# Linear attention, gated FFN and softmax attention on one core: another order of GpSimd's, SyncE's and VectorE's work at the borders of the stages

## The chip, the cores and the metric

One core of one Trainium2 chip. The metric is device microseconds of one execution of the whole program, as the median of several runs. Engines: TensorE (PE; PEld is its weight load), VectorE (DVE), ScalarE (ACT), GpSimd (POOL), SyncE (SP), which here only issues DMAs.

## What is computed

x has shape (8, 1024, 256). Four blocks follow each other, each with a residual: linear attention with 16 heads (softplus features, running sum of k v), an FFN, softmax attention with ALiBi bias and causal mask, the same FFN again. The FFN is one recurrent cell over the batch index, then a projection:

```python
x = x + linear_attention(layernorm(x))
x = x + ffn(layernorm(x))
x = x + softmax_attention(layernorm(x))
x = x + ffn(layernorm(x))

def ffn(x):                       # scan over x.shape[0] = 8 "steps", batch by batch
    for xt in x:                  # c: state, (1024, 256)
        ft = sigmoid(xt @ wf.T + c @ uf.T + bf)
        it = sigmoid(xt @ wi.T + c @ ui.T + bi)
        gt = tanh(xt @ wc.T + c @ uc.T + bc)
        c = ft * c + it * gt
    return tanh(x @ wo.T + c_final @ uo.T + bo)
```

The state c is carried from batch to batch, and what the FFN adds to any batch needs the state after the last one.

## The kernel before

There are two halves, "phase 1" (linear attention and first FFN) and "phase 2" (softmax attention and second FFN). Each is a software pipeline over the 8 batches: a stage is one value of b (from -2 to 8) and has 144 steps k. In stage b, attention runs on batch b, the projections of queries, keys and values on batch nb = b + 1, the FFN (output projection, second layer norm, gates of the recurrent cell) on batch pb = b - 1, and the first layer norm on batch fb = b + 2. Each engine has its own program with a fixed order, written out by hand; engines meet only at semaphores. An engine that waits holds up all that is behind it in its order.

Products are done in bf16 parts: a "high" part and a "low" part, which is the fp32 value less its high part. GpSimd makes most of the low parts, and they are what this change moves:

- `state_low` (L1630 to L1633): the low part of the state, 128x2048, after ACT's `state_high` (L1011, L1013). PE's first gate product of the next stage, at k = 68, waits for it (`state_split`).
- `chunks_low(b, half)` (L1654 to L1660): the low part of half of batch b's attention output, 128x1024. The second half waits for the last chunk, which DVE divides at k = 142 of stage b (`take_chunk`, L1376). PE wants it at k = 13 of stage b + 1, where it turns the attention output for the projection (L539).
- `layer_norm` (L1700): GpSimd's normalisations (L1696) and their low parts (`ln_low`, L1717). In phase 1 the second layer norm and the first of batches 0 and 1 are normalised by DVE (L1391), and GpSimd makes the low parts alone; in phase 2 it is batch 0 whose first layer norm is normalised by DVE.
- `split_q` (L1662), the masked queries of linear attention; `sum_h`, `add_h` (L1641, L1647), which add the first FFN to x at the start of phase 2, with a tanh of ACT between them (`tanh_h`, L1024); `qk_low` (L1676, L1678), parts of queries and keys; `split_max` (L1687, L1691), parts of the softmax maxima.

At the end of a stage DVE does, in this order, the division of the last chunk (L1376) and the gates of the last group (`gates`, L1230: L1236, L1238, L1240, each over 128x512 with two inputs in SBUF), then the masks of the next chunk's scores (L1356) and a copy of the turned layer norm (L1349). ACT does `state_high` at k = 143, once the gates are through, and then its own copy of the turned layer norm (L1073), for which PE waits with the next turning (both parts use the same two banks). GpSimd's order over a stage of phase 1:

```python
for b in range(-2, B + 1):
    nb, pb, fb = b + 1, b - 1, b + 2
    # chunks_low(pb, 1); layer_norm(1, 1) if fb == 1; split_q(nb, 0); layer_norm(1, 2, XR, pb);
    # split_q(nb, 1); layer_norm(1, 1, XA, fb); chunks_low(b, 0);
    # state_low(1, pb) if pb < B - 1       <- waits for the end of the stage
```

The last stage of phase 1, b = 8, has only the FFN of batch 7: turned attention output, projection, statistics (L1519), normalisation (L1391), four `ln_low`, then on DVE the splitting of two weights (`split_weights`, L1318 to L1323), gates, and the state's part of h (L559, L1280). Then DVE sets the state anew for the second FFN (`set_state`, L1325 to L1331: memset, two additions, cast, difference) and takes the statistics of batch 0 of phase 2 (L1481), whose additions GpSimd has done meanwhile (L1647).

In stage b = -1 of phase 2, PE projects queries, keys and values of batch 0 (L882, L893), ACT puts them into a two-row buffer (`qk_in`, L1112), GpSimd splits each row (`qk_low(0, r)`, r = 0 to 3), SP stores them to DRAM (`store_qk`) and loads them back as stacks of heads (`load_group(gg)`, four DMAs of 256 KB, L393). At k = 96 the scores of the first group begin: PE makes them (L716, L692) and DVE takes the maxima (L1409), 36 units a group; `combine` (L1416) closes a group, at k = 131 for group 0, then come `split_max`, a turning (L774), a copy and four small DMAs (L1101), and at k = 0 of stage 0 the exponentials of group 0 can begin. There PE also turns the layer norm of batch 1 (`turns`, L539), for which it waits until GpSimd's `ln_low` of batch 1 is through. SP's queue is in order too: `load_h` fetches what the first FFN has left of a batch's h and waits for `add_h` two chunks before; `load_x1(fb)` waits for the layer norm of batch fb - 1.

Of the kernel before, what the change touches and what calls it, by code (L numbers as in the profile page):

```python
# [13 lines left out]
B, T, D = 8, 1024, 256  # L14
# [118 lines left out]
def mixer_kernel(nc, x, weights, cols, rows, key_rows, masks, out):  # L133
    with ExitStack() as ctx:
# [165 lines left out]
        def _(sp):  # L300
# [161 lines left out]
            for b in range(-2, B + 1):  # L462
# [5 lines left out]
                if batch_in(b + 1):  # L468
                    store_qk(b + 1, 0)
                    store_qk(b + 1, 1)  # L470
                if batch_in(b + 2):
                    load_h(b + 2, 2)
                    load_h(b + 2, 3)
                if b == -1:
                    load_group(0)
                if b == B:
                    for n in (3, 4, 5):
                        load_final(n)
                if batch_in(b - 1):
                    store_residual(2, b - 1)  # L480
                if b == B:
                    for n in (1, 6):
                        load_final(n)
                if batch_in(b):
                    load_group(GROUPS * b + 3)
                if batch_in(b):
                    load_residual(2, b)
                if batch_in(b + 2):
                    sp.wait_ge(sem["h_added"], 4 * (b + 3))
                    sp.dma_start(tokens(x2_dram, b + 2), XA[:, :, :]).then_inc(sem["x2_out"], 16)  # L490
                if batch_in(b - 1):
                    store_xw(b - 1)
                if batch_in(b + 1) and b >= 0:
                    load_group(GROUPS * (b + 1))
                if batch_in(b + 1):
                    store_qk(b + 1, 2)
                    store_qk(b + 1, 3)
                if b == -1:
                    load_group(1)
                if batch_in(b + 3):  # L500
                    load_x1(b + 3)
                    load_h(b + 3, 0)
                    load_h(b + 3, 1)
# [490 lines left out]
        def _(act):  # L994
# [120 lines left out]
            def fill_softmax(b, k):  # L1115
# [7 lines left out]
                if batch_in(fb) and k in (5, 9, 33, 37) and (fb or k > 9):  # L1123
                    tanh_h(fb, (5, 9, 33, 37).index(k))
# [99 lines left out]
        def _(dve):  # L1224
# [236 lines left out]
            def fill_softmax(b, k):  # L1461
# [15 lines left out]
                if batch_in(fb):  # L1477
                    if 62 <= k < 70:
                        if k % 2 == 0:
                            dve.wait_ge(sem["h_added"], 4 * fb + (k - 62) // 2 + 1)  # L1480
                        i = dve.bn_stats(ST[:, k - 62, :], XA[:, k - 62, :])  # L1481
                        if k == 69:
                            step(i)
# [352 lines left out]
```

## Time and profile before

| | |
|---|---|
| median of 3 runs | 2644.91 us (2637.34, 2644.91, 2654.23) |
| the profiled execution's own time | 2651.77 us |
| its span, first to last instruction | 2649.9 us |
| TensorE busy | 2178.3 us, 82% |
| VectorE busy | 1706.4 us, 64% |
| ScalarE busy | 1256.1 us, 47% |
| GpSimd busy | 782.9 us, 30% |
| mean granted TensorE clock | 0.920 |

The runs differ by 0.6% among themselves. Times in rows are us from the start of the span. Phase 1 lasts until about 1078, phase 2 from there.

### The profile page before, as it was taken

To read this page: it belongs to the slowest core of one execution; us is meant where nothing else is said; L and a number is where in the kernel's file an instruction comes from. 1 tells how busy PE (TensorE), PEld (TensorE's weight loads), DVE (VectorE), ACT (ScalarE), POOL (GpSimd) and SP (SyncE) were. 2 spreads that over 40 slices of the span, in tenths; PEclk is the share of its full clock that TensorE was granted. 3 is DMA by queue.
4 is the path that set the end of the run, shared out by engine and by line. 5 is a ranking of instruction groups with operands and counts; after the bars stand their busy time and mean duration, and the time that the engine had idled before them with its cause. 6 is when DMAs were issued, how large, how long until landed. Compare 5 with 4: busy or idle time off the path is not lost.

```text
span 2649.9 us, 58583 instructions
## 1 busy us (share of the span) xinstructions
PE 2178.3 (82%) x24832; PEld 1226.0 (46%) x24832; DVE 1706.4 (64%) x3811; ACT 1256.1 (47%) x2025; POOL 782.9 (30%) x658
## 2 busy tenths in 40 slices
PE   3568988979898787478799989898999889988964
PEld 1346555655656554233244444444444434443432
DVE  5646565564655534477687687776877877677327
ACT  2414334243443221126566666666656656665623
POOL 2223331333231111352344243351532422312110
PEclk8789999899899897769899999999999999998977
DMA  3201020111101102243123132231332302213053
GB/s 94 64 17 49 17 65 17 49 33 33 49 1 49 33 17 72 79 118 101 55 81 113 43 109 76 81 113 34 97 98 58 105 25 73 73 34 103 27 222 127
DMA packets 133172, 179.29 MB, mean 68 GB/s; under 512 B 10752, under 2 KB 96768, under 8 KB 132912
## 3 DMA queue, kind: packets, MB, share of 16 engines
q1 hardware_dynamic: 128816, 175.02, 21.5%
q8 instruction: 196, 3.21, 0.5%
q10 hardware_dynamic: 4096, 0.53, 0.1%
q14 instruction: 64, 0.52, 0.1%
HBM read 97.40 MB, written 77.59 MB: 66 GB/s over the span
## 4 chain that ended last, share of the span: by engine, by line
PE 61%; DVE 22%; ACT 7%; issue 3%; ACTq 3%; POOL 2%; DMA 1%; SPq 0%; DVEq 0%; POOLq 0%
PE general L573 10%; PE general L882 9%; PE out_of_heads L760 9%; DVE maxima L1409 7%; PE scores L716 6%; PE general L559 4%; PE general L893 3%; ACTq L1101 3%; PE general L539 3%; PE turned_scores L730 3%; PE out_of_heads L647 3%; PE out_of_heads L657 2%; PE scores L605 2%; PE general L547 2%; ACT probs_turned L1080 1%
## 5 line engine op out<-in xcount | busy, mean ns | idle before, releaser
L1409 DVE TENSOR_REDUCE maxima<-scores 128x1 f32<-128x512 f32 (+3 forms) x1536 | 793.0, 552 | 314.2 <-PE scores L692 199.2
L1080 ACT ACTIVATE probs_turned<-turned_scores 128x512 f32<-128x512 f32 x1152 | 678.6, 601 | 476.3 <-PE turned_scores L692 206.7
L716 PE MATMUL scores<-k_stacks,q_stacks 59*128 59x512 bf16 (+3 forms) x1536 | 455.3, 343 | 81.1 <-DVE maxima L1409 75.0
L730 PE MATMUL turned_scores<-q_stacks,k_stacks 61*128 61x512 bf16 (+3 forms) x1536 | 446.2, 336 | 56.2 <-ACT probs_turned L1080 56.0
L716 PEld LDWEIGHTS scores<-k_stacks,q_stacks 59*128 59x128 bf16 x1536 | 126.0, 96 | 323.8 <-DVE maxima L1409 240.7
L1717 POOL TENSOR_TENSOR ln_low<-ln 128x512 bf16<-128x512 f32 x128 | 138.9, 1094 | 284.8 <-DVE ln L1391 261.7
L1696 POOL TENSOR_SCALAR ln<-x_for_attention,ln_mean_var,ln_rstd 128x256 f32<-128x256 f32 x104 | 128.4, 1246 | 204.6 <-DVEq L1488 114.1
L730 PEld LDWEIGHTS turned_scores<-q_stacks,k_stacks 61*128 61x128 bf16 x1536 | 127.3, 95 | 111.1 <-ACT probs_turned L1080 76.7
L1632 POOL TENSOR_TENSOR state_low<-state_doubled,state_high 128x2048 bf16<-128x2048 f32 x14 | 57.0, 4069 | 379.7 <-ACT state_high L1013 379.7
L760 PE MATMUL out_of_heads<-probs_turned,values_odd_and_heads_out 128*17 128x512 f32 (+3 forms) x1536 | 162.0, 518 | 1.3 <-ACT probs_turned L1080 1.3
L1007 ACT ACTIVATE gate_tanhs<-general,feature_vectors 128x512 f32<-128x512 f32 x96 | 66.0, 688 | 204.4 <-PE general L573 200.1
L760 PE MATMUL out_of_heads<-probs_turned,values 128*17 128x512 f32 (+3 forms) x1536 | 160.6, 514 | 0.0
L1374 DVE TENSOR_SCALAR reciprocals<-scores 128x16 f32<-128x16 f32 x64 | 11.1, 173 | 226.3 <-PE scores L665 226.3
L1048 ACT COPY values_odd_and_heads_out<-out_of_heads 128x512 f32<-128x512 f32 x64 | 37.5, 586 | 235.5 <-PE out_of_heads L657 233.8
L882 PE MATMUL general<-ln_turned_high,w_high 64*128 64x512 bf16 (+1 forms) x600 | 124.9, 381 | 24.8 <-ACT qk_block L1112 7.8
L692 PE MATMUL scores<-mask_scores,identity_halves_swapped 64*128 64x128 bf16 (+1 forms) x640 | 137.7, 215 | 0.0
L692 PE MATMUL scores<-mask_scores,identity 64*128 64x128 bf16 (+1 forms) x640 | 137.5, 215 | 0.0
L692 PE MATMUL turned_scores<-mask_turned,identity 64*128 64x128 bf16 (+1 forms) x640 | 135.3, 211 | 0.0
L692 PE MATMUL turned_scores<-mask_turned,identity_halves_swapped 64*128 64x128 bf16 (+1 forms) x640 | 135.2, 211 | 0.0
L1687 POOL CAST maxima_parts<-maxima 128x16 bf16<-128x16 f32 x64 | 10.6, 198 | 387.7 <-DVE maxima L1416 387.7
L882 PE MATMUL general<-ln_turned_low,w_high 64*128 64x512 bf16 (+1 forms) x600 | 123.8, 377 | 0.0
L882 PE MATMUL general<-ln_turned_high,w_low 64*128 64x512 bf16 (+1 forms) x600 | 123.4, 377 | 0.0
(240 smaller groups left out, 5512.8 us busy)
## 6 DMA issues: line engine op xcount, KB each, us to landing
x_after_attention<-x_residual SPq DMA_DIRECT2D x16, 1024.0 KB, 5.2
x_times_wo<-x_wo_out SPq DMA_DIRECT2D x64, 256.0 KB, 2.1
q_stacks<-q_stack SPq DMA_DIRECT2D x64, 256.0 KB, 4.6
k_stacks<-k_stack SPq DMA_DIRECT2D x64, 256.0 KB, 4.8
x_for_attention<-in_x SPq DMA_DIRECT2D x8, 1024.0 KB, 5.6
x_residual<-in_x SPq DMA_DIRECT2D x8, 1024.0 KB, 5.4
x_for_attention<-x_after_attention SPq DMA_DIRECT2D x8, 1024.0 KB, 5.6
ffn_h<-x_times_wo SPq DMA_DIRECT2D x32, 256.0 KB, 6.0
```

The costliest lines, as they stand in the source:

```text
L539: mm = pe.transpose(bank[:, :].bitcast(BF16)[:, n * P:(n + 1) * P], src, ident[:, :])
L559: mm = pe.matmul(bank[:, n * D:(n + 1) * D], src[xp][:, k, at], W[wp][:, m, k, :], start=(i == 0), stop=(i == len(todo) - 1))
L573: mm = pe.matmul(bank[:, :], W[wp][:, m, k, e * P:(e + 1) * P], src[xp][:, k, c * CH:(c + 1) * CH], start=(n == 0), stop=(n == len(todo) - 1))
L692: return pe.matmul(columns[:, first:last + 1:step, :], eye, m, start=False, stop=(n == 1))
L716: mx = pe.matmul(bank_s[:, first * P:(first + tiles) * P], QS[at_s:at_s + QROWS, r, i * P:(i + 1) * P], KS[at_s:at_s + QROWS, r, k0 * P:(k ...
L730: ex = pe.matmul(bank_t[:, first * P:(first + tiles) * P], KS[at_t:at_t + KROWS, r, j * P:(j + 1) * P], QS[at_t:at_t + KROWS, r, i0 * P:(i ...
L760: mm = pe.matmul(OB[half][32 * g:32 * g + HV, at:at + tiles * P], values[:, j, HV * h:HV * (h + 1)], PR[:, (HEADS * unit + g) % SLOTS, fir ...
L882: return pe.matmul(bank[:, :], W[wp][rows_, m, k, e * P:(e + 1) * P], src[xp][rows_, k, c * CH:(c + 1) * CH], start=start, stop=stop)
L1080: nc.scalar.activation(PR[:, s % SLOTS, :], TB[s % 2][:, :], ACT.Exp).then_inc(sem["ex_taken"], 1)
L1409: r = dve.tensor_reduce(MP[:, gg % 2, g, at:at + 1], max_bank[m][:, first * P:(first + tiles) * P], AX.X, ALU.max)
L1696: i = pool.tensor_scalar(XN[:, t, :], src[:, t, :], MV[:, which, t, 0:1], RS[:, which, t:t + 1], ALU.subtract, ALU.mult)
L1717: pool.tensor_tensor(pair(XL, c), pair(XN, c), top(pair(XN, c)), ALU.subtract).then_inc(sem[f"ln_low{phase}"], 1)
```

## The change

Five places.

1. GpSimd, phase 1: `state_low` leaves the end of the stage and comes one stage later, behind `split_q(nb, 1)`. The same seven calls remain.
2. DVE: `set_state` leaves the end of phase 1 and comes in stage -2 of phase 2 behind the normalisation of batch 0 (k = 78).
3. DVE: the statistics and Newton steps of batch 1 move from k = 62 to 76 of stage -1 to k = 110 to 124. ACT: the tanhs of chunks 2 and 3 of batch 1's h move from k = 33, 37 to 60, 61, behind the last `qk_in` (55).
4. GpSimd, stage -1 of phase 2: both `qk_low` of the first two rows in a row, then `add_h`, then the other two `qk_low`, then chunks 2 and 3 of h; the first `split_max` ahead of batch 1's layer norm instead of at the end.
5. SP, stage -1: `load_group(0)` ahead of `load_h(1, 2)` and `load_h(1, 3)`, and `load_group(1)` right behind these, ahead of the stores of rows 2 and 3.

```diff
 # SP, phase 2 (the old branch is kept for all b but -1)
                 if b == -1:
+                    store_qk(0, 0)
+                    store_qk(0, 1)
                     load_group(0)
+                    load_h(1, 2)
+                    load_h(1, 3)
+                    load_group(1)
+                    store_qk(0, 2)
+                    store_qk(0, 3)
+                    sp.wait_ge(sem["h_added"], 8)
+                    sp.dma_start(tokens(x2_dram, 1), XA[:, :, :]).then_inc(sem["x2_out"], 16)
+                    load_x1(2)
+                    load_h(2, 0)
+                    load_h(2, 1)
 # ACT
-                if batch_in(fb) and k in (5, 9, 33, 37) and (fb or k > 9):
-                    tanh_h(fb, (5, 9, 33, 37).index(k))
+                tanh_at = (5, 9, 60, 61) if fb == 1 else (5, 9, 33, 37)
+                if batch_in(fb) and k in tanh_at and (fb or k > 9):
+                    tanh_h(fb, tanh_at.index(k))
 # DVE, phase 2
-                    if 62 <= k < 70:
+                    at = k - 48 if fb == 1 else k
+                    if 62 <= at < 70:
...
+                    if k == 78 and fb == 0:
+                        set_state()
...
             state_part(1)
-            set_state()
 # GpSimd, phase 1
                 if batch_in(nb):
                     split_q(nb, 1)
+                if batch_in(pb - 1):
+                    state_low(1, pb - 1)
                 if batch_in(fb) and fb != 1:
                     layer_norm(1, 1, XA, fb)
                 if batch_in(b):
                     chunks_low(b, 0)
-                if batch_in(pb) and pb < B - 1:
-                    state_low(1, pb)
 # GpSimd, phase 2
-                if batch_in(nb):
+                if b == -1:
                     qk_low(nb, 0)
+                    qk_low(nb, 1)
                     add_h(fb, 0)
                     add_h(fb, 1)
+                    qk_low(nb, 2)
+                    qk_low(nb, 3)
                     for c in (2, 3):
                         sum_h(fb, c)
                     for c in (2, 3):
                         add_h(fb, c)
+                    split_max(0)
                     layer_norm(2, 1, XA, fb)
```

## Rows read from the trace of the kernel before

**Rows 1.** The page: chain that ended last by engine; one kind of DMA, us to landing.

```profile
PE 61%; DVE 22%; ACT 7%; issue 3%; ACTq 3%; POOL 2%; DMA 1%; SPq 0%; DVEq 0%; POOLq 0%
...
k_stacks<-k_stack SPq DMA_DIRECT2D x64, 256.0 KB, 4.8
```

**Rows 2.** The chain in order of time, border into stage 4: start, us, what.

```profile
535.65 0.42 DVE attention_out L1376
...
538.04 1.90 ACT state_high L1013
```

**Rows 3.** The timeline there: start, us, engine, line, operation [idle before it <- releaser].

```profile
536.00 0.68 DVE L1236 SCALAR_TENSOR_TENSOR gate_tanhs<-gate_tanhs,state_doubled 128x512 f32<-128x512 f32 x1
...
540.90 1.07 PE L539 MATMUL general<-identity,ln_low 128*128 128x128 bf16 x16 [2.40 <-ACT ln_turned_high L1073]
```

**Rows 4.** The timeline of stage 4: the last split_q and the first gate product.

```profile
591.65 2.85 POOL L1667 TENSOR_SCALAR state_part_of_h<-qk_block,mask_even_odd 128x1024 f32<-128x1024 f32 x1
...
601.82 0.38 PE L573 MATMUL general<-ln_turned_high,w_high 128*128 128x512 bf16 x1
```

**Rows 5.** The timeline at the border into stage 7.

```profile
886.71 4.06 POOL L1632 TENSOR_TENSOR state_low<-state_doubled,state_high 128x2048 bf16<-128x2048 f32 x1 [49.58 <-ACT state_high L1013]
...
892.68 1.04 PE L539 MATMUL general<-identity,attention_out 128*128 128x128 bf16 x8 [3.89 <-POOL attention_out_low L1659]
```

**Rows 6.** The timeline at the border into stage 8.

```profile
986.90 1.90 ACT L1013 CAST state_high<-state_doubled 128x2048 bf16<-128x2048 f32 x1 [2.63 <-DVE state_doubled L1240]
...
994.84 1.89 PE L539 MATMUL general<-identity,attention_out 128*128 128x128 bf16 x16 [10.85 <-POOL attention_out_low L1659]
...
995.91 1.01 ACT L1073 COPY ln_turned_high<-general 128x1024 bf16<-128x1024 bf16 x1 [7.11 <-PE general L539]
```

**Rows 7.** The timeline where GpSimd and DVE meet: stage 8, and phase 2.

```profile
1020.65 1.22 DVE L1323 TENSOR_TENSOR w_low<-qk_block,w_high 128x1024 bf16<-128x1024 f32 x1
...
1435.17 1.91 POOL L1651 TENSOR_TENSOR attention_out_low<-attention_out 128x1024 bf16<-128x1024 f32 x1
...
1435.87 1.75 DVE L1236 SCALAR_TENSOR_TENSOR gate_tanhs<-gate_tanhs,state_doubled 128x512 f32<-128x512 f32 x1
```

**Rows 8.** Stretches: us, busy per engine, then PEclk (granted clock), DMA share, GB/s.

```profile
896.00:900.00 4.00, 3.12 (x25) 2.02 (x27) 1.60 (x5) 1.01 (x1) 0.00 (x0) 0.50 0.00 0
...
1138.00:1174.00 36.00, 30.31 (x119) 11.46 (x119) 31.67 (x64) 0.26 (x1) 18.54 (x19) 0.50 0.52 140
```

**Rows 9.** The timeline at the border of the halves, DVE and GpSimd.

```profile
1078.74 1.76 DVE L1326 MEMSET state_doubled<- 128x2048 f32 x1 [0.49 <-DVE state_part_of_h L1280]
...
1079.55 2.94 POOL L1647 TENSOR_TENSOR x_for_attention<-x_for_attention,ffn_h 128x512 f32<-128x512 f32 x2
...
1092.49 4.83 DVE L1391 TENSOR_SCALAR ln<-x_for_attention,ln_mean_var,ln_rstd 128x256 f32<-128x256 f32 x8
...
1100.49 0.69 DVE L1349 COPY ln_turned_high<-general 128x1024 bf16<-128x1024 bf16 x1 [3.17 <-PE general L539]
```

**Rows 10.** The instructions of line 1328: ns min/median/max, first and last start.

```profile
L1328 DVE TENSOR_SCALAR state_doubled<-state_doubled,feature_vectors x4: 746/792/1745, 87.5 to 1081.3; 128x1024 f32<-128x1024 f32 x4
```

**Rows 11.** The timeline of stage -1, SP and PE.

```profile
1125.86 0.66 SPq L393 DMA_DIRECT2D q_stacks<-q_stack  x1
...
1130.96 1.01 PE L882 MATMUL general<-ln_turned_high,w_high 128*128 128x512 bf16 x2 [6.62 <-ACT qk_block L1112]
```

**Rows 12.** The timeline from the first maxima to the first turning of stage 0.

```profile
1137.86 2.68 DVE L1409 TENSOR_REDUCE maxima<-scores 128x1 f32<-128x512 f32 x4
...
1139.69 4.84 POOL L1696 TENSOR_SCALAR ln<-x_for_attention,ln_mean_var,ln_rstd 128x256 f32<-128x256 f32 x4
...
1151.33 2.04 POOL L1717 TENSOR_TENSOR ln_low<-ln 128x512 bf16<-128x512 f32 x2
...
1165.21 0.34 POOL L1687 CAST maxima_parts<-maxima 128x16 bf16<-128x16 f32 x2 [11.84 <-DVE maxima L1416]
...
1174.87 1.36 PE L539 MATMUL general<-identity,ln 128*128 128x128 bf16 x11
```

More of the change, by code:

```diff
@@ L479, in _ @@
[L479 to L498, printed above, removed]
-                    load_group(1)
[L500 to L503, printed above, removed]
+                    load_h(1, 2)
@@ new lines, in _ @@
+                    load_h(1, 3)
+                    load_group(1)
+                    store_qk(0, 2)
[5 more added lines that the diff above has]
+                    load_h(2, 1)
+                else:
+                    if batch_in(b + 1):
+                        store_qk(b + 1, 0)
+                        store_qk(b + 1, 1)
+                    if batch_in(b + 2):
+                        load_h(b + 2, 2)
+                        load_h(b + 2, 3)
+                    if b == B:
+                        for n in (3, 4, 5):
+                            load_final(n)
+                    if batch_in(b - 1):
+                        store_residual(2, b - 1)
+                    if b == B:
+                        for n in (1, 6):
+                            load_final(n)
+                    if batch_in(b):
+                        load_group(GROUPS * b + 3)
+                    if batch_in(b):
+                        load_residual(2, b)
+                    if batch_in(b + 2):
+                        sp.wait_ge(sem["h_added"], 4 * (b + 3))
+                        sp.dma_start(tokens(x2_dram, b + 2), XA[:, :, :]).then_inc(sem["x2_out"], 16)
+                    if batch_in(b - 1):
+                        store_xw(b - 1)
+                    if batch_in(b + 1) and b >= 0:
+                        load_group(GROUPS * (b + 1))
+                    if batch_in(b + 1):
+                        store_qk(b + 1, 2)
+                        store_qk(b + 1, 3)
+                    if batch_in(b + 3):
+                        load_x1(b + 3)
+                        load_h(b + 3, 0)
+                        load_h(b + 3, 1)
@@ L1747, in _ @@
                     out_low(pb, 1)
-                if batch_in(nb):
+                if b == -1:
                     qk_low(nb, 0)
-                if batch_in(fb):
+                    qk_low(nb, 1)
                     add_h(fb, 0)
                     add_h(fb, 1)
-                if batch_in(nb):
-                    qk_low(nb, 1)
-                if group_in(GROUPS * b + 1):
-                    split_max(GROUPS * b + 1)
-                if batch_in(fb):
+                    qk_low(nb, 2)
+                    qk_low(nb, 3)
                     for c in (2, 3):
@@ L1781, in _ @@
                     i.then_inc(sem["x2_biased"], 1)
-                if group_in(GROUPS * b + 4):
+                if group_in(GROUPS * b + 4) and b >= 0:
                     split_max(GROUPS * b + 4)
```

57 lines of the change are left out of this document (32 added, 25 removed).

## The prediction

> **What bounds the kernel now.** I read the page first: busy shares (the table above: TensorE 82%, GpSimd 30%), and the chain that ended last, 61% TensorE and 2% GpSimd [rows 1]. So no engine is short of hours on GpSimd; its work matters only where somebody waits for it, or where it holds somebody up. Then the chain in order of time across a stage border of the first half, and across the border of the halves. At a stage border the chain runs DVE gates, ACT `state_high`, ACT copy of the turned layer norm, PE turning [rows 2]: TensorE sits idle there 2.40 us behind ACT [rows 3]. At the last two borders of the first half TensorE waits for GpSimd instead, 3.89 and 10.85 us, because `state_low` (4.06) stands ahead of `chunks_low` (1.9, the rest of that wait) in GpSimd's order [rows 5, 6]. The border of the halves is one long chain in which every engine takes turns [rows 9, 12].
>
> All times below are of the profiled execution (2651.77 us with its start and end, span 2649.9), which lies 6.9 us above the median of the runs, 2644.91; I add the differences to the median.
>
> **Part 1: GpSimd takes the state's part later.** `state_low(1, b)` leaves the end of stage b+1 and runs in stage b+2, behind `split_q`, before gates that need it at k = 68. In a middle stage `split_q` ends at 594.5, `state_low` would end at 598.6, and PE's first gate product is at 601.82 [rows 4]: a cover of 3.2 us, so its new place costs nothing there. (If it were late, PE would stand at k = 68 with the whole fill behind it.) The other middle stages look alike.
>
> But with `state_low` gone from its front, `chunks_low(b, 1)` fires as soon as the last chunk is divided, and that is exactly when DVE begins the last three gate operations: the division ends at 536.07, the first gate operation issues at 536.00, and all three are through at 538.0, when ACT follows [rows 2, 3]. Does a GpSimd two-input operation hold up such a DVE one? The second half shows it five times with the same numbers: GpSimd's 1.91 us `out_low` begins at 1435.17, the first gate operation of DVE issues at 1435.87 and takes 1.75 us where the same one of rows 3 takes 0.68; it ends 0.5 us after GpSimd does [rows 7]. So DVE stood still until GpSimd was through. In the new order GpSimd asks while the first gate operation runs, gets its turn behind it, and the second one waits: 1.9 less some 0.15 by which the end of one and the start of the next overlap (in rows 7 DVE is through 0.54 behind GpSimd, though it needs 0.68), so 1.7 us. Then gates, `state_high`, ACT's copy and PE all come 1.7 us later, since nothing else is late in that chain [rows 2]. The bounds are 0 (GpSimd stands back until all three gates are through) and 1.9. I take 1.7. In the first half stages 2 to 6 begin with that chain: 5 x 1.7 = 8.5 us lost. Their `chunks_low` was hidden before, so they gain nothing.
>
> The Trainium skill ("SBUF — State Buffer", Who interferes with whom) calls the pair of ports that DVE and GpSimd share "an exclusive lock", held for the whole instruction, for a DVE operation with two SBUF inputs against a GpSimd one that reads SBUF. Rows 7 agree; by the rule alone the loss would be the full 1.9 a border, 9.5 us, and it speaks against this change.
>
> Longer idleness of TensorE (2.40 to 4.1 us a border) can also lose the clock: at the border into stage 7 it still had 0.50 of full speed, 1.2 GHz, from 896 to 900, after it had stood 3.89 us [rows 5, 8]. Bound: 0 to 4 us a border; I take 0.5, 2.5 us in all, because rows 8 follow longer idleness than the others will have.
>
> Stage 7's border: before, PE's turning began at 892.68, having been ready at 888.8 [rows 5]. Now it is ready 1.7 later (masks, too, stand behind the gates on DVE): 890.5. Gain 2.2.
> Stage 8's border: `chunks_low(7, 1)` starts near 985.4 and ends at 987.3, not 994.8. But PE's second turning needs ACT's copy, and ACT is in `state_high`, 1.90 us from 986.90 [rows 6], now from 988.6 to 990.5. The copy began at 995.91; it begins at 990.45. Gain 5.5.
> Then `state_low(1, 6)` falls behind the four `ln_low` of that stage, where DVE splits weights on the path: `w_low` (two SBUF inputs) issues at 1020.65, when GpSimd is just through with `ln_low`, its last before [rows 7]. GpSimd's 4.06 us now lie there, and by the reading above DVE stands till their end: 3.8 lost (bounds 0, where DVE goes first, and 4.1). Net of stage 8: 5.5 - 3.8 = 1.7 gained.
>
> **Part 2: the second state behind the first layer norm.** `set_state` ran for 7.9 us from 1078.74, with the statistics of batch 0 queued behind it, although the last addition of GpSimd was through by 1082.5 [rows 9], 1082.1 without that company. Statistics (8 x 0.34) now end at 1082.8 instead of 1089.25: 6.4 earlier. But `set_state` then stands between the normalisation and DVE's copy of the turned tile: 4.84 + 6.8 us (7.9 less the 1.0 by which GpSimd held up one of its steps, 1.745 instead of 0.75 [rows 10]), so the copy starts 11.6 after the normalisation's start where it started 8.0 after [rows 9]. Of 6.4, 3.6 are given back and 0.3 won in the second copy: products start 3.1 earlier, at 1100.35.
>
> **Part 3: the first keys ahead of batch 1's h.** GpSimd does both splits at once, so the second ends 4.8 earlier (3.1, and 1.7 because `add_h` no longer lies between). SP's `load_group(0)`, which wants those stores landed, goes from 1125.86 to 1121.1 [rows 11], ahead of `load_h`; its fourth part is issued 2.0 later and lands 4.8 after that [rows 1]: 1128. PE no longer waits 6.62 for ACT, which stood behind a tanh of h that waited for a DMA [rows 11]; it is ready at 1125. So the first maximum is taken at about 1129.0 instead of 1137.86 [rows 12]: 8.9 earlier. `load_h(1, 2..3)`, issued behind it, lands by 1132, its additions end by 1138, and nobody wants them before step 110.
> Then it is given back twice. Statistics and Newton steps of batch 1 (8 x 0.34 and 3.2 us) now lie among the maxima, of which DVE takes one each 0.75 us (36 in 27.1 us up to `combine` at 1164.97, just ahead of GpSimd's `split_max` [rows 12]); less what PE's 0.62 left open there, 4.2 us. So `combine` comes at 1129.0 + 27.1 + 4.2 = 1160.3, against 1164.97. And GpSimd's layer norm of batch 1, 13.7 us (1139.69 to 1153.4 [rows 12]), which lay under the maxima, now stands behind the first `split_max`: 1160.3 + 1.05 + 13.7 = 1175.1, where PE turned it at 1174.87 [rows 12]. PE will be ready at about 1171 and wait 4 to 6 us for GpSimd. Sum of parts 2 and 3: 0.3 lost (bounds: 5 gained, if PE's clock is full in the maxima, since 0.50 was granted there [rows 8]; 4 lost).
> Two stack loads in a row cost nothing: group 1 is read 36 steps after group 0. `load_x1(2)` and `load_h(2, 0)` wait for that layer norm and come some 22 us later; they land about 18.4 us after its start, just before ACT asks (19.7). Costed at nothing; a late one would stop exponentials behind a tanh.
>
> **Sum.** +8.5 + 2.5 (clock) - 2.2 - 1.7 + 0.3 = +7.4 us. From the median: 2652.3. That is +0.3%, and about 1% is what a measurement of this kernel can tell from no change.
>
> **Rivals.**
> A, GpSimd gives way. It waits for all three gate operations, so borders cost nothing (no clock loss either), stage 7 gains its whole 3.9, stage 8 gains 6.0 (its turning at 988.8), less 3.8, and 0.3 at the border of the halves: -5.8, 2639.1. For it: GpSimd asks when the second gate operation is queued with no wait. Against it: rows 7, where DVE waited.
> B, the border of the halves pays. Maxima at full clock and the layer norm earlier, -5 instead of +0.3, on top of the forecast's other terms: +2.1, 2647.0; on top of A: -11.1, 2633.8. Against it: 0.50 granted all through the maxima [rows 8].
> C, slower: the clock falls at every longer border. One mechanism: an idleness of 4.1 us in place of 2.40 lets the clock fall to 1.2 GHz, for half as long as rows 5 and 8 show (from 888 to 902), 7 us at each of five borders, of which half is lost where PE is the bound, 3.5 each, 17.5 instead of 2.5: +22.4, 2667.3. It decides once the stretch after a border shows half speed that it did not show before.
> D, the change doesn't do what it says: the layer norm of batch 1 isn't late, since maxima run slower; then parts 2 and 3 give back nothing more than DVE's 4.2: -4.7 instead of +0.3, 2647.3.
>
> **Chances.** Forecast 0.50, A 0.20, B 0.08, C 0.12, D 0.10. The range takes in A and C nearly whole, with the runs' own scatter: 2635 to 2667. Faster by over 1% (under 2618) wants A and B and more: 0.03. Slower by over 1% (over 2671) wants C with more: 0.04. Within: 0.93.
>
> **What would show it.** Right: the gate operations at the ends of stages 1 to 7 show one of about 2.4 us instead of 0.68 beside `attention_out_low`; `state_high` 1.7 later against the division; `w_low` in stage 8 at about 5 us; `set_state` behind the eight normalisations; a wait of PE for `ln_low` of 4 to 6 us at the first turning of the softmax half. Wrong: gates of 0.68 throughout (then A), or a first turning that waits for nothing (then B or D).

## The result, and the profile after

The changed kernel takes 2656.03 us (median of 9 runs, 2649.45 to 2668.44), the kernel before 2644.91: a ratio of 1.0044 [1.0026, 1.0062]. That is 11 us more, where 2652.3 was forecast, and inside the 1% that was called no change.

| | before | after |
|---|---|---|
| median of the runs | 2644.91 us | 2656.03 us |
| the profiled execution's own time | 2651.77 us | 2649.45 us |
| its span | 2649.9 us | 2647.4 us |
| TensorE, VectorE busy | 82%, 64% | 81%, 65% |
| mean granted TensorE clock | 0.920 | 0.926 |

The profiled execution of after is the fastest of its nine and that of before one of its slower ones, so the totals of the two profiles do not show the loss; their stages can be laid side by side, because each event is taken against the event that starts its stage.

**The stage borders.** The chain of waits of after, border into stage 4, in order of time (start, us, what):

```profile
543.22 0.43 DVE attention_out L1388
543.64 0.60 DVE gate_tanhs L1248
544.24 2.31 DVE gate_tanhs L1250
...
546.57 0.70 DVE state_doubled L1252
...
547.30 1.90 ACT state_high L1024
549.20 0.92 ACT ln_turned_high L1084
```

From the division of the last chunk (543.22) to `state_high` (547.30) it is 4.08 us, where it was 2.39 [rows 2]: 1.69 more. The timeline of after at the same place shows who stands in between (L1673 is `chunks_low`, L550 the turning):

```profile
543.72 2.27 POOL L1673 TENSOR_TENSOR attention_out_low<-attention_out 128x1024 bf16<-128x1024 f32 x1 [26.66 <-DVE attention_out L1388]
...
544.15 2.38 DVE L1250 SCALAR_TENSOR_TENSOR gate_tanhs<-gate_tanhs 128x512 f32<-128x512 f32 x1
...
550.17 1.10 PE L550 MATMUL general<-identity,ln_low 128*128 128x128 bf16 x16 [4.10 <-ACT ln_turned_high L1084]
```

GpSimd asks at 543.72, while the first gate operation runs; its record is 2.27 long instead of 1.89, because it waits for that one. Then the second gate operation waits for GpSimd: 2.38 instead of 0.68, and both end within 0.54 us (545.99, 546.53), as in [rows 7]. TensorE sits idle for 4.10 us where it sat 2.40 [rows 3]. The operation of 2.38 us is there at all seven stage ends and nowhere else.

But a stage became longer by more than that. The windows of the kernel before from one `state_high` to the next, first all five together, then one by one (us, busy time per engine, then the granted clock, DMA share, GB/s):

```profile
304.43:884.73 580.30, 509.73 (x6207) 343.70 (x6204) 339.12 (x778) 223.46 (x300) 175.72 (x103) 0.95 0.11 34
304.43:420.11 115.68, 101.52 (x1246) 68.11 (x1244) 68.99 (x162) 44.69 (x61) 38.03 (x23) 0.96 0.12 38
420.11:538.04 117.93, 104.26 (x1246) 70.40 (x1244) 68.98 (x162) 44.69 (x61) 38.02 (x23) 0.93 0.12 37
538.04:652.52 114.48, 99.97 (x1246) 67.39 (x1244) 68.99 (x162) 44.69 (x60) 38.04 (x23) 0.97 0.12 38
```

The same windows of the kernel after:

```profile
307.21:902.07 594.86, 508.32 (x6133) 349.44 (x6198) 347.80 (x778) 223.47 (x300) 177.49 (x103) 0.93 0.10 33
307.21:427.72 120.51, 103.48 (x1229) 71.41 (x1242) 70.72 (x162) 44.70 (x61) 38.37 (x23) 0.92 0.11 36
427.72:547.30 119.58, 102.43 (x1229) 70.40 (x1242) 70.72 (x162) 44.69 (x60) 38.38 (x23) 0.93 0.12 37
547.30:664.70 117.40, 99.82 (x1229) 68.12 (x1242) 70.73 (x162) 44.70 (x61) 38.39 (x23) 0.96 0.12 37
664.70:781.48 116.78, 99.30 (x1229) 68.41 (x1242) 70.71 (x162) 44.69 (x61) 38.39 (x23) 0.96 0.09 28
```

VectorE's busy time per stage rises by 1.73, GpSimd's by 0.35: the two engines standing at each other. The stage rises by 14.56 / 5 = 2.91 on average. What is left, 1.2 us a stage, comes together with a lower clock: 0.93 over the five stages instead of 0.95. It is no even loss. In either kernel a stage has one of a few lengths, and the longer ones have the lower clock (114.48 at 0.97, 115.68 at 0.96, 117.93 at 0.93; after: 116.78 and 117.40 at 0.96, 119.58 at 0.93, 120.51 at 0.92); the mix shifts.

**The last two stages of the first half** give back what was expected. In the timeline of after `chunks_low(7, 1)` is no longer behind `state_low`, but `state_low` now meets `w_low`:

```profile
998.73 1.89 PE L550 MATMUL general<-identity,attention_out 128*128 128x128 bf16 x16 [3.37 <-POOL attention_out_low L1673]
...
1025.03 4.51 POOL L1646 TENSOR_TENSOR state_low<-state_doubled,state_high 128x2048 bf16<-128x2048 f32 x1
...
1025.65 4.97 DVE L1335 TENSOR_TENSOR w_low<-qk_block,w_high 128x1024 bf16<-128x1024 f32 x1
...
1033.14 1.03 PE L550 MATMUL general<-identity,ln_low 128*128 128x128 bf16 x8 [4.85 <-DVE ln_turned_high L1361]
```

The wait of 10.85 [rows 6] is 3.37, with another of 2.23 for ACT's copy before the second turning; the 1.22 of `w_low` [rows 7] is 4.97, and TensorE now stands 4.85 us for what is queued behind it on VectorE. The first half ends 9.3 us later than before (last `state_part` at 1086.82 against 1077.49), where 7.1 was forecast. In pieces: 2.8 up to the first `state_high`, 14.6 over the five stages, -4.25 in stage 7 and -3.8 from there.

**The border of the halves**, timeline of after:

```profile
1095.39 4.84 DVE L1403 TENSOR_SCALAR ln<-x_for_attention,ln_mean_var,ln_rstd 128x256 f32<-128x256 f32 x8
...
1133.97 0.61 SPq L393 DMA_DIRECT2D k_stacks<-k_stack  x1
...
1140.94 0.61 PE L727 MATMUL scores<-k_stacks,q_stacks 59*128 59x512 bf16 x2 [5.55 <-DMA k_stacks<-k_stack]
...
1172.79 0.18 DVE L1428 TENSOR_TENSOR maxima<-maxima 128x16 f32<-128x16 f32 x1
...
1187.53 1.89 PE L550 MATMUL general<-identity,ln 128*128 128x128 bf16 x16 [4.77 <-POOL ln_low L1731]
...
1188.60 1.01 ACT L1084 COPY ln_turned_high<-general 128x1024 bf16<-128x1024 bf16 x1 [5.17 <-PE general L550]
```

Less the 9.3 of the first half: the normalisation begins at 1086.1 where it began at 1092.49 [rows 9], the first maximum (its matmul in row 3 of the fence) 5.6 earlier than in [rows 12], `combine` at 1163.5 just 1.5 earlier, and the first turning 3.3 later, behind a new wait of 4.77 us for GpSimd's layer norm of batch 1.

### The profile page after: what moved, and what is told of

Same layout as the page of the kernel before. It is cut to its first block, busy times and chain, and to the rows that moved or that the text cites. A ratio compares the mean times of both kernels' runs of the same rounds, so it can differ in the third digit from the quotient of the medians.

```text
span 2647.4 us, 58490 instructions
## 1 busy us (share of the span) xinstructions
PE 2152.1 (81%) x24731; PEld 1223.9 (46%) x24832; DVE 1718.0 (65%) x3811; ACT 1256.9 (47%) x2025; POOL 785.2 (30%) x658
## 4 chain that ended last, share of the span: by engine, by line
PE 59%; DVE 23%; ACT 7%; issue 4%; ACTq 3%; POOL 2%; DMA 1%; SPq 0%; DVEq 0%; POOLq 0%
PE general L893 9%; PE general L584 9%; PE out_of_heads L771 8%; DVE maxima L1421 7%; PE scores L727 5%; PE general L570 4%; PE general L904 3%; ACTq L1112 3%; PE general L550 3%; PE turned_scores L741 3%; PE out_of_heads L658 3%; PE out_of_heads L668 2%; PE scores L616 2%; PE general L558 2%; ACT probs_turned L1091 1%
## 5 line engine op out<-in xcount | busy, mean ns | idle before, releaser
L1386 DVE TENSOR_SCALAR reciprocals<-scores 128x16 f32<-128x16 f32 x64 | 11.1, 173 | 225.4 <-PE scores L676 225.3
L771 PE MATMUL out_of_heads<-probs_turned,values_odd_and_heads_out 128*17 128x512 f32 (+3 forms) x1536 | 154.1, 496 | 1.3 <-ACT probs_turned L1091 1.3
L570 PE MATMUL general<-w_high,ln_turned_high 128*128 128x256 bf16 x384 | 106.6, 278 | 16.0 <-DVE ln_turned_low L1361 9.7
```

Of the source, the lines that this page charges most:

```text
L570: mm = pe.matmul(bank[:, n * D:(n + 1) * D], src[xp][:, k, at], W[wp][:, m, k, :], start=(i == 0), stop=(i == len(todo) - 1))
L771: mm = pe.matmul(OB[half][32 * g:32 * g + HV, at:at + tiles * P], values[:, j, HV * h:HV * (h + 1)], PR[:, (HEADS * unit + g) % SLOTS, fir ...
```

## The experiments

Three things had to be told apart: which part carries the loss; whether it is GpSimd's hold on VectorE and not something else of part 1; and where the 1.2 us a stage come from that no queue explains. Ratios are against the kernel before on the same chip, in the same series. Of the ten kernels, two measure lateness by itself.

### Part 1 alone; the border of the halves alone

The kernel before, with only the three lines of part 1 on GpSimd:

```diff
                 if batch_in(nb):
                     split_q(nb, 1)
+                if batch_in(pb - 1):
+                    state_low(1, pb - 1)
...
-                if batch_in(pb) and pb < B - 1:
-                    state_low(1, pb)
```

> The kernel before with part 1 alone (state_low one stage later, nothing else). Theory (the port that GpSimd and VectorE share is held by chunks_low while the gates wait): at the end of stages 1 to 7 the second gate operation takes 2.38 us as in the changed kernel, six borders cost 1.7 us each, the waits of TensorE before stages 7 and 8 shrink; sum of phase 1 between +6 and +10 us, time about +7 against before. Rival (the loss sits at the border of the halves, part 1 pays for itself): -6, gates of 0.68.

The changed kernel with that undone:

> The changed kernel with state_low back in its old place. Theory: gates of 0.68 us, phase 1 as before; the border of the halves alone costs what the two traces show of it, TensorE's first turning of the softmax half 3.3 us later against the end of phase 1: +3 against before. Rival (part 1 is harmless): the whole +11 stays.

Part 1 alone: 2656.26 us, ratio 1.0036 [1.0024, 1.0049]. Without part 1: 2645.04 us, 0.9994 [0.9983, 1.0006]. Part 1 carries the whole loss; parts 2 and 3 together lie between -4.5 and +1.6 us, so the +3 expected from the two traces is not there in time. With part 1 alone the profile shows the 2.38 at all seven stage ends and five stages of 118.8 us on average, the longest four all 119.2 to 119.4 (a mix of its own, at 0.94 each and the short one at 0.96; the window over all five gives 0.95, as before, so two digits of mean clock don't carry the loss by themselves); without it no gate operation at a stage end is above 0.7 and the stages last 116.1.

### GpSimd waits for the gates

The changed kernel, in `chunks_low`:

```diff
                 pool.wait_ge(sem["o_taken1"], NT * bb + NT // 2 * (half + 1))
+                if half and bb:
+                    pool.wait_ge(sem["gate_used"], 4 * bb)
```

> The changed kernel, where chunks_low(b, 1) also waits until the gates of its stage are through (a wait added, nothing taken away). Theory: no gate operation over 0.7 us at a stage's end, the borders cost nothing again, stage 7 gains its 3.9 and stage 8 some 6 less 3.8 for the weights: about 15 us faster than the changed kernel, -4 against before. Rival (TensorE's longer idleness comes from elsewhere, for one the clock): no faster than the changed kernel.

2640.76 us, 0.9979 [0.9966, 0.9991]. The timeline of this kernel at the border into stage 4:

```profile
533.25 0.68 DVE L1250 SCALAR_TENSOR_TENSOR gate_tanhs<-gate_tanhs 128x512 f32<-128x512 f32 x1
533.97 0.69 DVE L1252 SCALAR_TENSOR_TENSOR state_doubled<-gate_tanhs 128x512 f32<-128x512 f32 x1
534.80 1.89 POOL L1675 TENSOR_TENSOR attention_out_low<-attention_out 128x1024 bf16<-128x1024 f32 x1 [28.65 <-DVE state_doubled L1252]
```

GpSimd begins 2.5 us behind the division instead of 0.5, and the kernel is 15 us faster than the changed one. TensorE's idleness at this border is 2.40 again. The stages are back at 115.9 us on average, with a clock of 0.95. So it was the meeting of the two engines; the wait makes by hand what rival A had GpSimd do by itself.

### The last state_low early as well

On top of it, the `state_low` that met `w_low` comes directly behind `chunks_low(7, 1)`:

```diff
+                if pb == B - 1:
+                    state_low(1, pb - 1)
...
-                if batch_in(pb - 1):
+                if batch_in(pb - 1) and pb < B - 1:
                     state_low(1, pb - 1)
```

> As the one with the wait for the gates, and the last state_low of phase 1 directly behind chunks_low(7, 1) instead of behind the four ln_low, so that it doesn't lie beside the splitting of weights. Theory (same port): w_low of that stage 1.2 us instead of 5, 3.8 us faster again: -8 against before. Rival (the splitting is hidden): no gain.

2634.46 us, 0.9959 [0.9944, 0.9974], 10.4 us by the medians below the kernel before and 6.3 below the kernel with the wait alone, where 3.8 was expected. The timeline of stage 8 in this kernel:

```profile
983.21 4.07 POOL L1646 TENSOR_TENSOR state_low<-state_doubled,state_high 128x2048 bf16<-128x2048 f32 x1
...
1009.00 1.23 DVE L1335 TENSOR_TENSOR w_low<-qk_block,w_high 128x1024 bf16<-128x1024 f32 x1
```

GpSimd's 4 us lie in a hole, `w_low` is at 1.23 again, and the wait of TensorE behind it is 1.10 instead of 4.85.

### What the border of the halves is worth once GpSimd is out of the way

The kernel before with part 1 in this mended form, its border of the halves untouched:

> The kernel before with part 1 alone, mended in both places (chunks_low waits for the gates, the last state_low directly behind the last chunks_low); the border of the halves as before. Theory (the border's change is worth nothing either way: -0.0006 when it was alone): the same time as the changed kernel so mended, 2634.5, -10 against the kernel before, within 2 us. Rival (the border costs the 3 us that the trace of the changed kernel shows at the first turning): 2631.5. Rival on the other side (the border brings something once GpSimd is out of the way): 2638.

2635.13 us, 0.9958 [0.9945, 0.9972]: the same as with the changed border (2634.46), within what these runs tell. ACT's copy of the first turned tile starts 98.3 us behind the start of the last `state_part` here, 98.45 in the kernel before and 100.7 with part 1 alone; with the changed border it is 98.1 to 101.8 in seven kernels. The spread within either group (2.4 and 3.7 us) is larger than the distance of their means.

The changed border with its own flaw mended, the statistics of batch 1 nine maxima earlier and its layer norm ahead of the first `split_max`:

```diff
-                    at = k - 48 if fb == 1 else k
+                    at = k - 39 if fb == 1 else k
...
-                    split_max(0)
                     layer_norm(2, 1, XA, fb)
+                    split_max(0)
```

> The changed kernel with GpSimd's chunks_low waiting for the gates and the last state_low early (as in the run before this one), and in the border of the halves the statistics of batch 1 nine maxima earlier and its layer norm ahead of split_max(0). Theory (the layer norm of batch 1 behind split_max ends last there: TensorE waited 4.76 us for ln_low at its first turning in that run): the statistics end about 7.5 us earlier (near 1137 instead of 1144.4), the layer norm takes 13.7 us and ends near 1151, split_max starts about 1.2 us later than before, and the first turning comes at about 1160.5 instead of 1164.3, with no wait for ln_low: 3 to 4 us less than that run, so 2631, -14 against the kernel before. Rival: what follows the border is paced by DVE, which has the same work either way: the first turning is earlier, and the time stays at 2634, -10. Second rival: GpSimd's normalisations beside the maxima slow the maxima and split_max comes over 4 us later: 2636.

2634.97 us, 0.9961 [0.9949, 0.9974]. A miss: no gain over the kernel without this edit, and ACT's copy of the first turned tile starts 100.5 us behind the last `state_part` against 99.6. TensorE's timeline says why, and GpSimd's ahead of it:

```profile
1139.28 4.83 POOL L1712 TENSOR_SCALAR ln<-x_for_attention,ln_mean_var,ln_rstd 128x256 f32<-128x256 f32 x4 [13.30 <-DVEq L1501]
...
1152.88 0.33 POOL L1703 CAST maxima_parts<-maxima 128x16 bf16<-128x16 f32 x2
...
1163.76 0.60 PE L741 MATMUL turned_scores<-q_stacks,k_stacks 61*128 61x512 bf16 x1 [2.84 <-DMA q_stacks<-maxima_rows]
...
1164.40 1.89 PE L550 MATMUL general<-identity,ln 128*128 128x128 bf16 x16
```

The layer norm ended at 1152.9 instead of the 1151 expected, `split_max` began 3.1 us later than in the kernel without the edit (1149.80), and what hangs on it, the transfer of the maxima into the stacks, came late in turn: TensorE was ready at 1160.9 and waited 2.84 us for that. The wait for `ln_low` was replaced by one for `split_max`. Both are on one engine and 13.7 us of layer norm have to go somewhere; the order chose who waited. Not all of the lateness is the edit's: behind the last `state_part` the first maximum itself came 2.5 us later here (55.1 against 52.6), and the first stack load took 7.0 us to its matmul against 5.3. With a load as quick as in the other kernel the edit might have gained; that isn't shown.

### The hold in four pieces

The changed kernel, with each `chunks_low` in four instructions of 128x256:

```diff
-                src = flat(ON[:, NT // 2 * half:NT // 2 * (half + 1), :])
-                pool.tensor_tensor(flat(OL[:, NT // 2 * half:NT // 2 * (half + 1), :]), src, top(src), ALU.subtract
-                                   ).then_inc(sem["o_low1"], 1)
+                for n in range(NT // 2 * half, NT // 2 * (half + 1)):
+                    i = pool.tensor_tensor(OL[:, n, :], ON[:, n, :], top(ON[:, n, :]), ALU.subtract)
+                i.then_inc(sem["o_low1"], 1)
```

> The changed kernel with each chunks_low in four instructions of 128x256 instead of one of 128x1024; nothing waits for the gates. Theory (DVE stands for as long as the one GpSimd instruction runs that holds the ports, and the two alternate between instructions): the gate operations behind the first take about 1.1 to 1.2 us each (0.68 and one piece of some 0.55) instead of one of 2.38; two pieces fall between them, so state_high comes about 1.1 us late instead of 1.7, and 5 borders give back some 3 us: 2653. Rival (GpSimd's queue keeps the ports over all its instructions): still one gate operation of about 2.4 or more, 2656 or above. Rival (GpSimd gets a turn only when DVE has nothing queued once instructions are short): gates of 0.68, and 2647.

2642.09 us, 0.9992 [0.9979, 1.0005], 14 us below the changed kernel where 3 were expected. Its timeline at the border into stage 4:

```profile
539.69 0.68 DVE L1248 SCALAR_TENSOR_TENSOR gate_tanhs<-gate_tanhs,state_doubled 128x512 f32<-128x512 f32 x1
539.85 3.60 POOL L1673 TENSOR_TENSOR attention_out_low<-attention_out 128x256 bf16<-128x256 f32 x4 [26.23 <-DVE attention_out L1388]
540.29 1.10 DVE L1250 SCALAR_TENSOR_TENSOR gate_tanhs<-gate_tanhs 128x512 f32<-128x512 f32 x1
541.42 0.99 DVE L1252 SCALAR_TENSOR_TENSOR state_doubled<-gate_tanhs 128x512 f32<-128x512 f32 x1
```

The engines alternate instruction by instruction: GpSimd's four pieces (2.32 us together where nobody is beside them) are spread over 3.60, and each of two gate operations stands for one piece, 0.42 and 0.30 us. From division to `state_high` it is 3.10 us, so only 0.7 late, not 1.1. The hold is that of one instruction, as the theory said. But the stages last 116.6 us on average, 2.4 less than in the changed kernel, for 1.0 us less of lateness. So most of the 11 us beyond the expected 3 is not the hold but something that comes with it; the clock over the five stages is 0.95 here, and whether lateness by itself does this was the open question.

### Lateness without GpSimd

The kernel in which GpSimd waits for the gates, with work of VectorE's own in the place of the hold: 3 reductions, and in a second kernel 2.

```diff
                 dve.scalar_tensor_tensor(out=first, in0=first, scalar=1.0, in1=cs,
                                          op0=ALU.add, op1=ALU.mult)
+                if phase == 1 and group == 3:
+                    for i in range(3):
+                        dve.tensor_reduce(MP[:, 0, 0, i:i + 1], TG[:, 2, 0:480], AX.X, ALU.max)
```

> The changed kernel with chunks_low waiting for the gates (a stage of the first half then lasts 115.9 us on average from state_high to state_high, against 119.0 in the changed kernel), and three reductions of 480 columns on VectorE behind the first gate operation at the end of each stage: about 1.7 us of VectorE's own work in the place where GpSimd's instruction held it. Theory (what the change costs is 1.7 us at each border as seen by VectorE, and the rest of the 3 us a stage is TensorE's clock after the longer idleness): stages last 118.5 to 119.3 us, the first twentieth of a stage shows a granted clock near 0.65 on average, and the time is 2655, +14 against the kernel with the wait. Rival (only the 1.7 us: the other 1.2 us come from something that GpSimd does beside the gates): stages of 117.6 us, 2649.

> The same with two such reductions instead of three: about 1.1 us, as late as in the kernel with chunks_low in four pieces. Theory (the clock's part has a step between 1.1 and 1.7 us of lateness: in the kernel in four pieces four of five stages kept 0.73 to 0.76 in their first twentieth and lasted 116.1 us): stages of 116.1 to 116.6 us on average and 2643 to 2646. Rival (the clock's part grows evenly with the lateness): stages of 117.9 us, 2651.

With three: 2656.87 us, 1.0035 [1.0019, 1.0052]. With two: 2644.95 us, 0.9992 [0.9973, 1.0010]. The windows over the same five stages, the kernel with three first:

```profile
308.67:903.07 594.40, 507.80 (x6133) 349.19 (x6198) 347.62 (x793) 223.48 (x301) 175.64 (x103) 0.93 0.10 33
```

and the kernel with two, with two of its stages:

```profile
307.36:888.00 580.64, 495.95 (x6133) 341.66 (x6198) 344.86 (x788) 223.47 (x301) 175.66 (x103) 0.96 0.11 34
...
423.68:539.80 116.12, 99.27 (x1229) 68.46 (x1242) 70.13 (x164) 44.70 (x60) 38.02 (x23) 0.96 0.12 38
539.80:655.88 116.08, 99.25 (x1229) 68.40 (x1242) 70.14 (x164) 44.70 (x61) 38.01 (x23) 0.96 0.12 38
```

GpSimd's busy time is 175.6 in both, as in the kernel before: it meets nobody. And still three reductions cost the whole 14 us that the changed kernel loses over these stages. Six kernels in one table, by how late `state_high` comes behind the division (2.39 in the kernel before):

| lateness, us | made by | idle of TensorE at the border | mean stage, us | clock | time, us |
|---|---|---|---|---|---|
| 0 | kernel before | 2.40 | 116.06 | 0.95 | 2644.9 |
| 0 | wait for the gates | 2.40 | 115.91 | 0.95 | 2640.8 |
| 0.7 | GpSimd in four pieces | 3.11 | 116.57 | 0.95 | 2642.1 |
| 1.1 | two reductions | 3.52 | 116.13 | 0.96 | 2645.0 |
| 1.7 | three reductions | 4.08 | 118.88 | 0.93 | 2656.9 |
| 1.7 | the change | 4.10 | 118.97 | 0.93 | 2656.0 |

The other kernels fit in: the six without lateness have mean stages of 115.8 to 116.4 us, the four with 1.7 us of it 118.8 to 119.2. So two reductions leave the stage within what no lateness gives, and the next 0.6 us cost 2.8 a stage: it is no even price. With 3.5 us of idleness all five stages are alike, 116.0 to 116.3 at 0.96, and those of 117.9 at 0.93 are gone. The rival of an even growth expected 2651 from two reductions and fell. In time, against the kernel with the wait (0.9979), two reductions cost 0.13%, which the intervals can't tell from nothing, and three 0.56%.

Where in a stage the clock is lost shows in twentieths of it. Windows of one stage with three reductions (first, second, eighth, ninth and tenth twentieth):

```profile
543.40:549.40 6.00, 2.92 (x21) 2.74 (x23) 3.57 (x7) 4.85 (x4) 1.89 (x1) 0.64 0.00 0
549.40:555.40 6.00, 6.00 (x50) 2.70 (x50) 0.40 (x2) 2.96 (x5) 0.00 (x0) 0.79 0.01 3
...
585.60:591.60 6.00, 1.34 (x28) 1.08 (x32) 5.86 (x14) 1.64 (x2) 0.32 (x1) 0.82 0.00 0
591.60:597.60 6.00, 4.86 (x66) 3.33 (x62) 4.55 (x8) 0.96 (x2) 5.31 (x5) 0.50 0.13 29
597.60:603.60 6.00, 5.66 (x60) 4.97 (x56) 2.74 (x5) 2.03 (x2) 6.00 (x3) 0.54 0.43 148
```

and of one with two, the same twentieths:

```profile
423.70:429.50 5.80, 2.90 (x20) 2.72 (x22) 3.37 (x6) 4.66 (x4) 1.89 (x1) 0.71 0.00 0
429.50:435.30 5.80, 5.70 (x54) 3.01 (x55) 0.61 (x2) 4.10 (x6) 0.00 (x0) 1.00 0.01 3
...
464.30:470.10 5.80, 0.90 (x20) 0.74 (x24) 5.66 (x13) 1.88 (x2) 0.00 (x0) 0.73 0.01 3
470.10:475.90 5.80, 4.65 (x76) 3.24 (x72) 5.00 (x10) 0.96 (x2) 4.99 (x5) 0.68 0.08 16
475.90:481.70 5.80, 4.79 (x75) 4.16 (x68) 4.41 (x8) 2.05 (x3) 5.80 (x3) 1.00 0.53 170
```

In all 60 stages of the twelve kernels the clock is below 1.00 in these two places only: behind the border (the first tenth), and in the middle, where in the two stages shown TensorE is busy for 1.34 of 6.00 or 0.90 of 5.80 us. The expected 0.65 of the first twentieth is a miss: with three reductions it is 0.57 to 0.83, 0.71 on average, and 0.71 with two as well. The two kernels differ in the second twentieth (0.88 against 1.00 on average) and in the middle, where three of five stages fall to 0.50 and none with two reductions below 0.67. So the dearer stages lose their clock half a stage behind the late border too, and not only right after it.

A rough estimate of what that is worth: the time at half speed (twice the missing share of each twentieth) is 11.6 us a stage in the kernel before, 10.2 with two reductions, 15.7 with three and 15.7 in the change, and half of such time is lost at most. That leaves room for 2.0 us a stage in the change, where 1.2 is to be explained, but with part 1 alone (12.9 us) only for 0.7, where 1.1 is. With two reductions it gives back at most 0.7 of the delay of 1.1. Shown is that the dear stages of a kernel are those with the lower clock. Whether the clock is the whole of what the hold leaves unexplained isn't, nor how the lateness of a border brings about the fall in the middle.

### The two stack loads in a row

The changed kernel with `load_group(1)` back behind the stores of rows 2 and 3, as before the change. One run.

```diff
                     load_h(1, 2)
                     load_h(1, 3)
-                    load_group(1)
                     store_qk(0, 2)
                     store_qk(0, 3)
+                    load_group(1)
```

> The changed kernel with load_group(1) back behind the stores of the third and fourth part, as it stood in the kernel before; so the first stack load has only load_h behind it. Theory (two loads in a row cost nothing): TensorE's wait for k_stacks at the first scores stays at 5.55 us within 0.5, and the first maximum is as far behind the end of phase 1 as in the changed kernel (54.8 us behind the start of the last state_part_of_h). Rival (the second load's packets lie among the first one's and delay its landing): that wait falls to 3.5 to 4 us, and the first maximum comes 1.5 to 2 us earlier.

2655.2 us in one run. TensorE's timeline:

```profile
1140.47 0.61 PE L727 MATMUL scores<-k_stacks,q_stacks 59*128 59x512 bf16 x2 [2.78 <-DMA k_stacks<-k_stack]
```

2.78 instead of 5.55, and the first maximum 52.0 us behind the last `state_part` instead of 54.8: on this the rival would have won. But eight other kernels with both loads in a row show how much it varies. Their wait at this place is 2.33 and 2.64 (with the reductions), 3.58 (wait for the gates), 4.24 (without part 1), 4.42 (last `state_low` early), 5.36 (four pieces), 5.55, 5.70. From the issue of the last part of the first load to the matmul it is 5.1 to 5.4 us in four of them and 6.6 to 7.0 in the other four; here 5.3. A single run can't be told from this spread, and whether the second load delays the first stays open; by these two profiles its price would be 2.8 us.

## Why the prediction was right, and where it wasn't

Right in its sum (+7.4 forecast, +11.1 measured) and in its main mechanism, with the clock's term mis-sized. The sum came out a little better than its terms, which is luck: in the profiles the five stages are 3.6 us over the forecast, what lies before them 1.1 and the border of the halves 3.0, while stages 7 and 8 are 2.4 under it; and the profiles add up to +12.6, the medians to +11.1.

- **The hold at the borders, 1.7 us each.** Forecast 2.4 for the held gate operation and `state_high` 1.7 later; measured 2.38 and 1.69 at every border. Rows of the other half of the kernel, with another output form, gave the size to 0.02. Rival A fell: GpSimd doesn't stand back, it takes its turn between two of VectorE's instructions.
- **The clock, forecast 2.5 us in all.** This step failed in size. I took 0.5 a border because [rows 8] follow a longer idleness; over the five stages what the hold leaves is 14.56 - 5 x 1.69 = 6.1 us, 1.2 a border, and no other cause of it is known. Rival C had 3.5 a border for the same mechanism. What I missed was already in the trace of before: stages of 114.5, 115.7 and 117.9 us with equal work, each with its own clock, which warn that a delay may have no fixed price. The runs with reductions show that price jump between 1.1 and 1.7 us, and the change lies beyond the jump. The first `state_high` is 2.78 us later than before, 1.1 more than the hold; in the eight profiles without a hold of 1.7 us, or with less of it, it lies anywhere from 303.3 to 307.9.
- **Stage 7.** Forecast -2.2 between the two `state_high` of it, measured 97.92 against 102.17: -4.25. The wait went as forecast, and the half speed behind it [rows 5, 8] went too: the clock of this stage is 0.94 instead of 0.88. I had priced the clock where idleness grew and not where it shrank.
- **Stage 8.** Forecast -3.4 from `state_high` to the last `state_part`, net of `w_low`; measured 86.8 against 90.6, -3.8. `w_low` at 4.97 (forecast about 5), and the run with an early `state_low` shows this term as one of its own.
- **Part 2.** The normalisation 6.4 earlier, as forecast (1086.1 against 1092.5), and the copy of the turned tile at 1098.0 against a forecast of 1097.7.
- **Part 3.** The mechanism was right: maxima 8.9 earlier by the forecast, then 4.2 us of statistics among them (first maximum to `combine` 31.2 us, forecast 31.3), then the layer norm behind `split_max`, a wait of 4.77 (forecast 4 to 6). Of the profiled run the size was off by 3 us in one term: the first maximum is 5.6 us earlier, not 8.9. The stores landed 7.5 us behind the issue of the last one where before they took 6.7, and the first load took 7.0 to its matmul where I had 4.8 to its landing. Over the kernels of the study these two vary from 6.0 to 8.1 and from 5.1 to 7.0 us: I gave a transfer's time as one number where it has a spread of two. At the first turning the profiled run stands at +3.3 instead of +0.3, the six others with this border in its own order at -0.3 to +3.1; in time, the run without part 1 (0.9994) shows nothing. D and B, which had 4.7 and 5 us of gain there, lie just outside that interval (-4.5), and their mark, a first turning that waits for nothing, is in no run of this border in its own order. The forecast of next to nothing stands.

The edit that was costed at nothing (`state_low` behind `split_q` in the middle stages) did cost nothing: no wait for it shows, and the kernels that keep it and wait for the gates are the fastest.

**The fastest kernel** of the study is the change with the wait for the gates and the last `state_low` early: 2634.46 us, 10 us below the kernel before and 22 below the change. The kernel before with only part 1 so mended is as fast within what the runs tell (2635.13), so parts 2 and 3 are not needed for it. Its gain is that of stages 7 and 8, which the change had aimed at and then paid for at every other border.

## What to carry to other kernels

When you take work off the front of an engine's queue, look at what fires in its place, and at which instructions of the other engine it then meets; a wait for something that is done a microsecond later can be worth more than the early start. Where equal stages have unequal lengths in the trace of before, and each length has its own clock, a small delay may have no fixed price: measure it with a delay of the engine's own, at two sizes. And an engine's last call in a loop may sit in front of other work than all its calls before; price it by itself.

## What the runs showed of the hardware

- GpSimd and VectorE take turns by instruction. A GpSimd subtraction of two f32 inputs (128x1024, 1.89 us alone) that is asked for while VectorE has three operations queued runs between the first and the second; in four pieces, it alternates, and VectorE loses 0.42 and 0.30 us to pieces of 0.58. This fits what the Trainium skill ("SBUF — State Buffer", Who interferes with whom) says of an exclusive lock for the whole instruction; when both have work queued, neither is kept out here.
- The price of TensorE's idleness at a border has a step. Beside the kernel with the wait for the gates (0.9979 of the kernel before), 1.1 us more of idleness at each border cost 0.13% (0.9992), and 1.7 us 0.56% (1.0035; 2656.87 against 2644.95 us, 12 us for the last 0.6 a border). Such a step was one of the two outcomes named for these runs, but not in the prediction.
- The granted clock falls below full speed in the same two places in all 60 stages laid out: behind the border, and in the middle, where in the stages shown TensorE had been busy for 1.34 of 6.00 and 0.90 of 5.80 us.
- The time from the issue of the last store to that of the load that waits for it is 6.0 to 8.1 us over twelve profiles, for the same transfers.
